# Copies of key and query tiles ahead of sines and folds in a linear-attention kernel on one core

## The reference

```python
def _fourier_kernel(x, proj_mat):
    p = jnp.einsum('blhd,dm->blhm', x, proj_mat) / math.sqrt(D_HEAD)
    return jnp.concatenate([jnp.cos(p), jnp.sin(p)], axis=-1) / math.sqrt(D_KMAP)
q = (x @ Wq.T + bq).reshape(Bv, Lv, N_HEAD, D_HEAD)      # 16 heads of 32
k = (x @ Wk.T + bk).reshape(Bv, Lv, N_HEAD, D_HEAD)
v = (x @ Wv.T + bv).reshape(Bv, Lv, N_HEAD, D_HEAD)
kv = jnp.einsum('blhm,blhd->bhmd', _fourier_kernel(k, proj_mat), v)
out = jnp.einsum('blhm,bhmd->blhd', _fourier_kernel(q, proj_mat), kv)
return out.reshape(Bv, Lv, D_MODEL) @ Wo.T + bo
```

## Time and profile before

| what | us |
|---|---|
| median of three runs | 1628.83 (1627.93 to 1632.57) |
| the profiled execution | 1629.87 |
| its span, first to last instruction | 1627.5 |
| PE busy, whole span | 1564.6 |
| DVE busy | 1208.0 |
| ACT busy | 1113.9 |
| POOL busy | 715.5 |

### The profile page before, as it was taken

How to read it: one execution, slowest core, us unless ns; L and a number is a source line. 1 busy time by engine, 2 the same in 40 slices (tenths; PEclk the granted TensorE clock), 3 DMA queues, 4 the chain that set the end, 5 groups by cost and what they waited for, 6 DMA issues and landing times. The chain is left out here.

```text
span 1627.5 us, 29746 instructions
## 1 busy us (share of the span) xinstructions
PE 1564.6 (96%) x11188; PEld 1116.4 (69%) x11188; DVE 1208.0 (74%) x1849; ACT 1113.9 (68%) x1450; POOL 715.5 (44%) x633
## 2 busy tenths in 40 slices
PE   8999999999999999999999999999799999999996
PEld 6756765676676667667667766765478888888884
DVE  5687577668767766876776687898687777877876
ACT  5796677678667767867777786668256655565664
POOL 4233115203412410340232044373288978898886
PEclk9999999999999999999999999999899999999998
DMA  5100102201210220120022022001512222222211
GB/s 173 53 27 28 52 1 79 79 1 36 83 39 1 79 79 2 52 81 25 1 79 79 2 66 89 30 27 52 150 49 85 85 78 84 84 79 83 78 40 65
DMA packets 49175, 95.75 MB, mean 59 GB/s; under 512 B 3552, under 2 KB 3872, under 8 KB 49056
## 3 DMA queue, kind: packets, MB, share of 16 engines
q1 hardware_dynamic: 39776, 76.67, 15.0%
q10 hardware_dynamic: 9280, 17.31, 2.9%
HBM read 60.38 MB, written 33.59 MB: 58 GB/s over the span
## 5 line engine op out<-in xcount | busy, mean ns | idle before, releaser
L793 DVE SCALAR_TENSOR_TENSOR feat<-feat,phases 128x1024 f32<-128x1024 f32 x256 | 300.9, 1217 | 167.2 <-ACT feat L683 167.1
L683 ACT ACTIVATE feat<-phases 128x1024 f32<-128x1024 f32 x256 | 248.4, 1024 | 127.3 <-PE phases L533 108.2
L690 ACT ACTIVATE feat<-feat 128x1024 f32<-128x1024 f32 x256 | 271.7, 1062 | 74.8 <-DVE feat L793 66.0
L396 POOL TENSOR_TENSOR xt_hi<-xt_raw,singles 128x512 fp32r<-128x512 f32 x60 | 67.7, 1158 | 481.1 <-PE bank L525 451.0
L696 ACT ACTIVATE feat<-feat 128x1024 f32<-128x1024 f32 x256 | 257.2, 1046 | 8.8 <-DVE feat L800 8.4
L800 DVE TENSOR_SCALAR feat<-feat 128x1024 int32<-128x1024 int32 x256 | 209.6, 823 | 45.8 <-ACT feat L690 45.3
L418 POOL TENSOR_TENSOR res<-res,bo_all 128x512 f32<-128x512 f32 x60 | 75.5, 1283 | 211.0 <-DMA res<-x 210.7
L595 PE MATMUL kv_sum<-feat,v 128*32 128x256 f32 x2048 | 123.8, 382 | 0.0
L621 PE MATMUL kv_sum<-feat,kv_cols 128*32 128x512 f32 x1024 | 123.1, 598 | 0.0
L523 PE MATMUL bank<-xt_hi,win_hi 128*128 128x512 f32 x256 | 108.3, 423 | 7.9 <-DVE win_lo L745 7.9
L1305 ACT ACTIVATE xs<-xs,shift,rstd 128x512 f32<-128x512 f32 x96 | 71.5, 807 | 63.4 <-POOL shift L1168 63.4
(11 more groups left out here) (219 smaller groups left out, 3611.6 us busy)
## 6 DMA issues: line engine op xcount, KB each, us to landing
normed<-res SPq DMA_DIRECT2D x32, 513.0 KB, 4.2
xt_raw<-xT SPq DMA_DIRECT2D x15, 1024.0 KB, 7.3
res<-x SPq DMA_DIRECT2D x30, 512.0 KB, 4.2
xs<-normed SPq DMA_DIRECT2D x24, 513.0 KB, 3.9
out<-xs ACTq DMA_DIRECT2D x24, 512.0 KB, 2.8
feat<-normed SPq DMA_DIRECT2D x8, 513.0 KB, 3.8
out<-feat ACTq DMA_DIRECT2D x8, 512.0 KB, 2.8
xt_raw<-ctx SPq DMA_DIRECT2D x8, 256.0 KB, 3.6
```

The lines of the kernel that those rows point to most:

```text
L683: act.activation(feat[2 * (w % 2) + p][:, 0, :], phases[:, 2 * p:2 * p + 2, :].rearrange("p h n -> p (h n)"), ACT.Identity, bias=ROUND).th ...
L690: act.activation(f[:, 1, :], f[:, 0, :], ACT.Sin, scale=-TWO_PI).then_inc(sin_done, 1)
L793: dve.scalar_tensor_tensor(f[:, 0, :], f[:, 0, :], ROUND, phases[:, 2 * p:2 * p + 2, :].rearrange("p h n -> p (h n)"), ALU.subtract, ALU.s ...
```

## The change

In `attention_steps`, the step `K` or `Q` of a slot moves from behind `sin` to ahead of it. This is done in all 16 slots of the main list, in slot 2 of the list for the first batch (whose slots from 3 on come from the main list; its slots 0 and 1 stay as they are), and in slots 12 and 13 of the list for the tail. No instruction is added or removed, and the lists of PE, SP and POOL are the same as before, since `sin` issues nothing there.

```diff
-        11: [sin(11), Q(1, 1), cos(11), norm(1, 0), norm(1, 1), V(0, 0), out(10)],
-        12: [sin(12), Q(1, 2), cos(12), V(0, 1), out(11)],
-        13: [sin(13), Q(1, 3), cos(13), W(0, 0), W(0, 1), out(12)],
-        14: [sin(14), K(0, 0), cos(14), W(0, 2), W(0, 3), stats(0), out(13)],
...
+        11: [Q(1, 1), sin(11), cos(11), norm(1, 0), norm(1, 1), V(0, 0), out(10)],
+        12: [Q(1, 2), sin(12), cos(12), V(0, 1), out(11)],
+        13: [Q(1, 3), sin(13), cos(13), W(0, 0), W(0, 1), out(12)],
+        14: [K(0, 0), sin(14), cos(14), W(0, 2), W(0, 3), stats(0), out(13)],
...
-        8: [sin(8), Q(0, 2), cos(8), kv(7), turned(0), save(1)],
-        9: [sin(9), Q(0, 3), cos(9), W(1, 3), out(8), turned(1), stats(1)],
+        8: [Q(0, 2), sin(8), cos(8), kv(7), turned(0), save(1)],
+        9: [Q(0, 3), sin(9), cos(9), W(1, 3), out(8), turned(1), stats(1)],
...
-        2: [sin(2), K(1, 0), cos(2), V(1, 1), kv(1)],
+        2: [K(1, 0), sin(2), cos(2), V(1, 1), kv(1)],
...
-        12: [sin(12), Q(1, 2), cos(12), out(11)],
-        13: [sin(13), Q(1, 3), cos(13), W(0, 0), out(12)],
+        12: [Q(1, 2), sin(12), cos(12), out(11)],
+        13: [Q(1, 3), sin(13), cos(13), W(0, 0), out(12)],
```

More of the change, by code:

```diff
@@ L112, in attention_steps @@
     after = {
-        11: [sin(11), Q(1, 1), cos(11), norm(1, 0), norm(1, 1), V(0, 0), out(10)],
-        12: [sin(12), Q(1, 2), cos(12), V(0, 1), out(11)],
-        13: [sin(13), Q(1, 3), cos(13), W(0, 0), W(0, 1), out(12)],
-        14: [sin(14), K(0, 0), cos(14), W(0, 2), W(0, 3), stats(0), out(13)],
-        15: [sin(15), K(0, 1), cos(15), V(0, 2), norm(0, 0), out(14), norm(0, 1)],
-        0: [sin(0), K(0, 2), cos(0), V(0, 3), out(15)],
-        1: [sin(1), K(0, 3), cos(1), V(1, 0), kv(0)],
-        2: [sin(2), K(1, 0), cos(2), V(1, 1), kv(1)],
[L121 to L125, removed]
-        8: [sin(8), Q(0, 2), cos(8), kv(7), turned(0), save(1)],
-        9: [sin(9), Q(0, 3), cos(9), W(1, 3), out(8), turned(1), stats(1)],
-        10: [sin(10), Q(1, 0), cos(10), out(9)],
+        11: [Q(1, 1), sin(11), cos(11), norm(1, 0), norm(1, 1), V(0, 0), out(10)],
+        12: [Q(1, 2), sin(12), cos(12), V(0, 1), out(11)],
+        13: [Q(1, 3), sin(13), cos(13), W(0, 0), W(0, 1), out(12)],
+        14: [K(0, 0), sin(14), cos(14), W(0, 2), W(0, 3), stats(0), out(13)],
+        15: [K(0, 1), sin(15), cos(15), V(0, 2), norm(0, 0), out(14), norm(0, 1)],
+        0: [K(0, 2), sin(0), cos(0), V(0, 3), out(15)],
+        1: [K(0, 3), sin(1), cos(1), V(1, 0), kv(0)],
+        2: [K(1, 0), sin(2), cos(2), V(1, 1), kv(1)],
+        3: [K(1, 1), sin(3), cos(3), V(1, 2), kv(2)],
+        4: [K(1, 2), sin(4), cos(4), V(1, 3), kv(3)],
+        5: [K(1, 3), sin(5), cos(5), W(1, 0), kv(4)],
+        6: [Q(0, 0), sin(6), cos(6), W(1, 1), kv(5)],
+        7: [Q(0, 1), sin(7), cos(7), save(0), W(1, 2), kv(6)],
+        8: [Q(0, 2), sin(8), cos(8), kv(7), turned(0), save(1)],
+        9: [Q(0, 3), sin(9), cos(9), W(1, 3), out(8), turned(1), stats(1)],
+        10: [Q(1, 0), sin(10), cos(10), out(9)],
     }
```

## The result

The changed kernel takes 1603.8 us (median of 4 runs, 1603.43 to 1605.24) against 1630.7 us beside it (4 runs, 1627.93 to 1635.82): ratio 0.9833, 95% interval [0.9812, 0.9854]. The forecast was 1613.5 with a range down to 1607, so the direction was right and the gain, 26 to 27 us, was well above the 15.4 forecast and outside the range.

A forecast was written before the change was run, and what follows sets the result against it. PE's own work was the floor, so only its waits could be won: 12.0 + 1.2 + 3.5 + 0.6 + 2.0 - 3.9 = 15.4 us off 1629.87 gives 1614.5, predicted as a median of 1613.5 us; range 1607 to 1624.

The forecast's parts named there:

- those in slots 12, 13 and 14: PE's bank waits before Q(1,2), W(0,1) and W(0,3) go, winning 1.2, 12.0 and 3.5 us.
- Rival B: W(0,1) gets its bank but PE stops as much later in slot 14 or at a W bank; 1627 us, chance 0.11.
- Rival A: Phase 11 held the full 1.2 us in six batches, first and last batch win nothing; 1619.3 us, chance 0.20.
- Rival C: Slower: lateness grows through slots 9 to 11, 4.1 us a batch; 1637 us, chance 0.11.
- the give-back of -3.9 us in the six loop batches: Slots 8 to 11: waiting `stack_hi` delays ACT and DVE, so phase 11 comes 0.65 us later in each batch.
- the 2.0 us of slot 9 counted as nothing: Six waits before transpose L608, 1.6 us idle, go but give nothing, since PE then waits 2 us later.
- the last cosine and `att_hi` come 1.2 us later: Slot 9: late fractions, `stack_lo` ahead and folds of 3.02 us beside GpSimd's split delay these by 1.2 us.
- The 0.54 of ACT's lateness: Slot 8's cosines end 0.54 us later because `stack_hi` waits for Q's product, so slot 9's rounds start later.
- a wait that swallows part of a delay: L855 before slot 11's phases: about 1.0 of its 1.24 us is waiting, swallowing most but not all lateness.
- the surcharge per wait, 0.16 us: Each PE wait that goes returns 0.16 us beyond its shown idle time, read in slot 13.
- the first batch, 0.6 forecast: Slots 8 to 10: fractions of slot 10 end near 106.3, phase 11 started at 106.93; 0.6 us won, bounds 0 and 4.9.
- the last batch, 2.0 forecast: Slots 8 to 10 and tail: the wait of 1.97 us goes, next Q product 2.0 us earlier; bounds 0 and 3.7.

The follow-up runs named there:

- DVE alone: Changed kernel with ACT's loop put back in the old order, so only DVE has the new one: 1687.38 us, ratio 1.0347 against the kernel before.
- Slots 8 to 10 alone: Kernel before with only Q(0,2), Q(0,3) and Q(1,0) moved ahead of their sines: 1622.77 us, ratio 0.995.
- keys only: Kernel before with only the K steps moved ahead of the sines, Q steps left behind them: 1624.66 us, ratio 0.9961.
- ACT alone: Changed kernel with DVE's loop put back in the old order, so only ACT has the new one: 1642.73 us, ratio 1.0068 against the kernel before.

## Why the prediction was wrong

*Right.* PE's waits bound the first part, and those in slots 12, 13 and 14 went as forecast: 16.7 forecast, 18.8 measured. The second part did not move. Rival B (the wait only moves) is out, since W(0,1)'s own starts came the forecast 12.0 us earlier in sum. Rival A, a larger give-back, falls with the give-back itself. Rival C needed lateness that grows, and the stretch from phase 8 to phase 11 became shorter instead, 21.03 us against 21.45 to 21.49 in every loop batch. DVE alone shows what such lateness costs when it does occur.

*Wrong: the give-back of -3.9 us in the six loop batches, and the 2.0 us of slot 9 counted as nothing (5.9 of the 11.2 us by which the ledger exceeds the forecast).* The step that failed is "the last cosine and `att_hi` come 1.2 us later". They came 0.07 later. Two inputs of it were off. The 0.54 of ACT's lateness left out that the sines, started later, no longer stop between their halves (2.19 with a pause before, 1.99 now). And the folds were given the 3.02 us of before, twice 1.51, at their new place. The rows after, GpSimd and DVE in 649 to 650 us:

```profile
648.00 3.03 POOL L396 TENSOR_TENSOR xt_hi<-xt_raw,singles 128x512 fp32r<-128x512 f32 x2
...
648.61 1.53 DVE L800 TENSOR_SCALAR feat<-feat 128x1024 int32<-128x1024 int32 x1
```

The second fold still takes 1.53. The first, which stands 0.6 ahead of it at 648.01, starts where GpSimd goes from one instruction to the next and takes 0.69, as it does alone; it is the GpSimd instruction beside it that is long, 1.59 us against 1.04 for the one before. At the end L855 was taken as a wait that swallows part of a delay; before, it had missed the end of a GpSimd instruction by 0.06 us, so that a small shift the other way caught it. That shift came: GpSimd's four start 0.10 behind PE's phases of slot 10 now and 0.33 ahead of them before (651.12 and 651.02, against 665.42 and 665.75), 0.43 apart, of which 0.33 is the L608 wait that went. Slots 8 to 10 alone, 7 us faster, shows that there was no give-back. The stated range missed this as well: its low end of 1607 took the best case of the first and the last batch, but left the give-back at 3.9 us. With the prediction's own smaller bound of 0.6 there it would have begun at 1604.

*Wrong: the surcharge per wait, 0.16 us.* It was read at the restart alone, where it held. The next step behind a pause wins 0.13 to 0.18 more, so that the surcharge is 0.30. Over 14 pauses that is +1.9 us.

*Wrong: the first batch, 0.6 forecast, 2.3 measured.* The forecast carried its chain of slots 8 to 10 over to there. The fractions of slot 10, expected 1.3 us later than 102.65, start at 102.10, and the phases give back 0.75 instead of nearly all. Without the two pauses the clock stays high (0.92 before, 1.00 now), but the 1.6 us of it are not kept. The wait of 1.7 us shown above takes them: the output of slot 9 starts at 102.28 in the timeline, right behind DVE's copy of `kv_cols` (101.50 to 102.18).

*Wrong: the last batch, 2.0 forecast, 3.5 measured.* The slow clock went, with all of the 1.6 us named as a bound: from 1056 to 1067 us it is 1.00 now. PE comes 1.87 us earlier by W(1,1) and W(1,2), whose waits for `res` the forecast did not count. Of all this 2.05 us was given back later in the tail.

One cause runs through the first of these: a copy was charged at its full length to the engine that carries it, though both engines had pauses between fraction, sine and fold into which it fits in part. That the same shortening of the chain explains the shorter waits of slot 13 in the kernels that moved nothing there (keys only, slots 8 to 10 alone) is argued, not shown, and so is any share of chance in them. In the last batch PE gives back 0.71, 0.30 and 0.93 us in slots 10, 11 and 12 and 0.63 at a transpose of the tail, in waits for `res` and for fractions; what made those late was not followed up.

## What to carry to other kernels

Before pricing an instruction that moves on an engine, look at whether it lands where the engine waits for its partner in a chain (here 0.37 to 0.43 us between halves): there a copy of 0.7 us costs less than its length. Here both engines' copies had to move together; one side alone was 11 and 56 us slower. Where one instruction seems to wait for another engine's instruction to end, price a shift as a step: look how far past the last boundary it starts; here a shift of 0.27 us moved its end by a whole instruction, 1.25 us. And take a PE pause at its cost two steps on, not at its idle time, and look at the granted clock behind it: where the clock fell, a wait of 1.6 to 2.2 us cost 1.6 more.

## What the runs showed of the hardware

A VectorE instruction of four elements a partition, 0.17 us alone, takes up to 1.25 us and ends within 0.03 us of where a GpSimd instruction ends, in each of the six loop batches of the kernel before. Not every instruction is held up so. Groups of the changed kernel over the whole span, folds and low parts: shortest, median and longest in ns.

```profile
L800 DVE TENSOR_SCALAR feat<-feat x256: 678/690/1784, 21.5 to 1113.6; 128x1024 int32<-128x1024 int32 x128
```

```profile
L814 DVE SCALAR_TENSOR_TENSOR stack_lo<-bank,columns,stack_hi x64: 744/747/752, 76.6 to 1094.9; 128x512 fp32r<-128x512 f32 x64
```

The folds, from SBUF to SBUF, go up to 2.6 times their median, while the low part, one of whose inputs is in PSUM, never takes more than 0.75 us, also at 647.35, in the middle of GpSimd's split. The Trainium skill, GPSIMD Engine Reference, section "8. Key points", says that GpSimd shares its SBUF interfaces with VectorE and that the two contend where VectorE is in a two-port mode or has two SBUF inputs. The folds agree with the first half, by these numbers; which of the two conditions held for L855 no run here shows. The GpSimd side pays too: in the changed kernel's fold at 648.01, which starts with a GpSimd instruction and not in the middle of one, the fold takes its usual 0.69 us and GpSimd's L396 1.59 instead of 1.04.

PE's clock was 0.92 in the stretch with the two pauses of 1.42 and 1.55 us, and 1.00 once they were gone: matmuls that had been 0.43 apart are 0.23 apart. In the last batch 1.6 us came the same way. A pause alone does not tell whether the clock falls. In ACT alone it fell behind slot 13's pauses of 2.11, 2.22, 2.01 and 1.87 us and not behind those of 2.17, 1.90 and 2.46; in the kernel before, not behind the 2.12 us of its second batch.
